# Routed experts of a gated two-layer block: expert blocks loaded transposed as fp16 halves, three sets of PSUM banks, spacing steps left out between scatters, and a new written order

## The reference

```
x = x + tanh(gx0) * decayed_scan(ln(x) * ctx * ctx)              # "A", by one matmul with a decay matrix
x = x + tanh(gf0) * (ln(x) @ W.T + top-1 of 4 low-rank adapters)  # "B"
x = x + tanh(gx1) * sigmoid_attention(ln(x), ctx) @ Wo            # "C", 16 heads of 16 features
x = x + tanh(gf1) * moe(ln(x))                                    # "E"
# moe: logits = x2 @ router_w (8 experts); each token goes to its best 2 experts;
#      h = gelu(row @ w_in[e] + b_in[e]);  y = h @ w_out[e] + b_out[e];  y is weighted and added
```

## Time and profile before

| | us |
|---|---|
| median of three runs | 473.06 |
| lowest and highest | 472.47, 476.5 |
| the profiled execution, device time | 474.49 |
| its span, first to last instruction | 472.6 |
| busy in the span: PE, DVE, ACT, POOL | 394.9, 368.8, 331.4, 268.7 |

### The profile page before, as it was taken

One profiled execution on the slowest core, in us unless ns is written; L12 is line 12 of the kernel. 1 busy time (PEld: TensorE's weight loads), 2 busy tenths in 40 slices (PEclk: granted clock), 3 DMA queues, 4 the chain that ended last, 5 costly groups with the idle time before them and its releaser, 6 DMA issues.

```text
span 472.6 us, 13099 instructions
## 1 busy us (share of the span) xinstructions
PE 394.9 (84%) x4092; PEld 308.3 (65%) x4092; DVE 368.8 (78%) x1416; ACT 331.4 (70%) x671; POOL 268.7 (57%) x313
## 2 busy tenths in 40 slices
PE   2758899998999989999899987789559999979850
PEld 1536667776776777677686765568438897967740
DVE  2888888998988889899789786367655667779994
ACT  2855788898889889898879877566706666646640
POOL 2522112545454364626545565769988888888870
PEclk9998999999999999999999999899959999999996
DMA  7245576664565555875553774624335569396985
GB/s 242 83 139 163 180 214 179 196 181 141 177 213 170 166 171 167 221 204 184 180 174 111 223 220 121 198 68 130 101 126 143 170 175 332 116 341 251 323 275 204
DMA packets 69500, 87.10 MB, mean 184 GB/s; under 512 B 9485, under 2 KB 55290, under 8 KB 69306
## 3 DMA queue, kind: packets, MB, share of 16 engines
q1 hardware_dynamic: 60074, 65.81, 46.7%
q0 software_dynamic: 6816, 18.65, 10.8%
q10 hardware_dynamic: 2544, 1.81, 1.2%
HBM read 51.07 MB, written 35.18 MB: 182 GB/s over the span
## 4 chain that ended last, share of the span: by engine, by line
PE 42%; POOL 17%; issue 14%; DVE 10%; DMA 8%; ACT 6%; ACTq 0%; POOLq 0%; DVEq 0%; SPq 0%
PE ps_J L1650 12%; PE ps_F L1650 6%; POOL store_y L771 6%; DMA store_y<-y_out,y_row 6%; PE ps_O L1764 5%; PE ps_T L1659 5%; POOL store_x L765 5%; PE ps_S L1751 5%; POOL pause_t L778 5%; PE ps_R L1689 2%; PE ps_O L1775 2%; PE ps_G L1650 2%; DMA temp_t<-in_temp 1%; DVE y_out L2934 1%; DVE xb_lo L2903 1%
## 5 line engine op out<-in xcount | busy, mean ns | idle before, releaser
L771 POOL DMA_INDIRECT store_y<-y_out,y_row x78 | 81.4, 1044 | 21.8 <-issue 16.5
L765 POOL DMA_INDIRECT store_x<-xn_E,slot_u x64 | 68.0, 1063 | 26.5 <-DVE slot_u L2633 13.6
L1089 ACT ACTIVATE prob<-ps_S 128x512 f32<-128x512 f32 x128 | 72.4, 594 | 12.7 <-PE ps_S L1751 10.0
L778 POOL TENSOR_TENSOR pause_t<-half_ones,minus_half 128x2 f32<-128x2 f32 x71 | 54.7, 770 | 1.9
L1751 PE MATMUL ps_S<-q_stack,k_stack 128*128 128x256 f16 x256 | 44.5, 276 | 5.9 <-issue 3.8
L2922 DVE TENSOR_TENSOR h_lo<-h_f,h_hi 128x512 f16<-128x512 f32 x39 | 26.9, 689 | 21.0 <-ACT h_hi L1173 9.4
L1650 PE MATMUL ps_J<-wout_hi,h_hi 128*128 x112 | 31.2, 278 | 14.3 <-DVE y_out L2934 10.9
L1764 PE MATMUL ps_O<-prob,v_wide 128*32 128x128 f32 x1024 | 41.0, 279 | 1.1 <-ACT prob L1089 0.5
L1165 ACT ACTIVATE h_f<-ps_F,bin_t 128x256 f32<-128x256 f32 x56 | 23.4, 470 | 24.5 <-PE ps_F L1650 18.9
L751 POOL TENSOR_TENSOR rstd_C<-var_C,minus_half 128x2 f32<-128x2 f32 x16 | 12.1, 759 | 40.4 <-DVE var_C L2412 40.4
L1650 PE MATMUL ps_F<-xb_hi,win_hi 128*128 128x256 f16 x112 | 31.7, 283 | 3.9 <-DVE xb_lo L2903 3.3
(11 more groups left out here) (301 smaller groups left out, 1399.5 us busy)
## 6 DMA issues: line engine op xcount, KB each, us to landing
parts_scratch<-parts SPq DMA_DIRECT2D x32, 256.0 KB
k_stack<-parts_scratch SPq DMA_DIRECT2D x64, 128.0 KB
q_stack<-parts_scratch SPq DMA_DIRECT2D x128, 64.0 KB
xb<-store_x SPq DMA_DIRECT2D x30, 257.0 KB
y_got<-store_y SPq DMA_DIRECT2D x14, 512.0 KB
c_in<-in_ctx SPq DMA_DIRECT2D x16, 256.0 KB
x_in<-in_x SPq DMA_DIRECT2D x16, 256.0 KB
store_x<-zeros SPq DMA_DIRECT2D x15, 257.0 KB, 4.6
```

The lines of the kernel that those rows point to most:

```text
L765: pool.indirect_dma_start(store_x, bass.IndirectOffsetOnAxis(slot_u[q][:, at:at + 1], 0), xn_e[q][:, at, :], None).then_inc(s_scat[q], 16)
L771: pool.indirect_dma_start(store_y, bass.IndirectOffsetOnAxis(y_row[n][:, b:b + 1], 0), y_out[n][:, b, :], None).then_inc(s_y_kept[n], 16)
L778: pool.tensor_tensor(pause_t[:, :], half_ones[:, :], minus_half[:, 0:2], ALU.pow).then_inc(s_set_p, 1)
L1089: act.activation(prob[m % PROBS][:, 2 * n:2 * n + 2, :, :], bank_s[n], ACT.Sigmoid, scale=float(HD) ** -0.5).then_inc(s_prob[n], 1)
```

## The change

**Rows as fp16 parts.** xn_E keeps its 1028-byte rows, but now 512 fp16 values (256 hi, 256 lo) stand in them in place of 256 fp32 values, and the row number stays in the last column. ScalarE's `rows_hi(p)` takes the place of its `normed_e(p)` (same elements, fp16 out). VectorE gets a new `normed_e(p)`, the fp32 rows once per token, into a single buffer xn_f that `transpose_e` reads. GpSimd gets `rows_lo(p)`, 1024 elements per partition, and every scatter waits for it:

```diff
+            def rows_lo(p):
+                pool.wait_ge(s_rows_hi, 2 * p + 2)
+                pool.wait_ge(s_xn["E"], 2 * p + 2)
+                pool.tensor_tensor(e_lo[p % 2], xn_f[:, :, :].unsqueeze(2).broadcast_to([128, 2, TOP, D]), e_hi[p % 2],
+                                   ALU.subtract).then_inc(s_rows_lo, 1)
...
+            def normed_e(p):
+                q = p % 2
...
+                dve.wait_ge(s_rstd["E"], p + 1)
+                need(dve, s_t["E"], p)
+                need(dve, s_rows_lo, p)
+                for b in range(2):
+                    dve.tensor_scalar(xn_f[:, b, :], xs[:, 2 * p + b, :], mv["E"][q][:, b, 0:1], rstd["E"][q][:, b:b + 1],
+                                      ALU.subtract, ALU.mult).then_inc(s_xn["E"], 1)
```

**Transposing block loads.** `load_block` issues two transfers; `transpose_block`, `copy_hi` and `copy_lo` are gone, and `layer1` reads the loaded tile:

```diff
-                sp.dma_start(xb[n][:, :, :], store_x[bass.ds(row_at(i, 0), BLK), :]
-                             .rearrange("(p b) c -> p b c", b=SUB))\
-                    .then_inc(s_xb[n] if n < XB else s_late[(n - XB) // GROUP], 16)
+                at, done = row_at(i, 0), s_xb[n] if n < XB else s_late[(n - XB) // GROUP]
+                sp.dma_start(xb[n][:, :, :], store_x16[bass.ds(at, BLK), 0:2 * D], transpose=True).then_inc(done, 16)
+                sp.dma_start(row_no[n][:, :, :], store_x[bass.ds(at, BLK), D - 1:WIDE].rearrange("(b p) c -> p b c", b=SUB))\
+                    .then_inc(done, 16)
```

**Spacing steps.** From the first `keep_block` on, 6 of 43 are left. The new order on GpSimd there:

```diff
+            keep_block(1, 0)
+            keep_block(1, 1)
+            rows_lo(15)
+            keep_block(2, 0)
+            keep_block(2, 1)
+            keep_block(3, 0)
+            scatter(15, 3)
+            scatter(15, 0)
+            long_pause()
+            scatter(15, 1)
+            keep_block(3, 1)
+            keep_block(4, 0)
+            long_pause()
+            long_pause()
+            keep_block(4, 1)
...
+            keep_block(7, 0)
+            scatter(15, 2)
+            long_pause()
+            keep_block(7, 1)
```

More of the change, by code:

```diff
@@ L413, in build, with last_at @@
         block = st.enter_context(nc.Block())
+        store_x16 = store_x.bitcast(F16)
         def side(i):
-            return 0 if i <= EARLY else (i - EARLY) % 2
+            return i % HB
+        def last_at(k):
+            return max(i for i in range(TILES) if side(i) == k)
         def home(i):
@@ L718, in _ @@
             stack_keys(15)
+            keep_parts("q", 15)
             load_block(0)
+            stack_queries(15)
             load_block(1)
[L721 to L732, removed]
+            load_block(2)
@@ L1637, in _ @@
-            for b in range(2):
-                keep_batch(NP - 1, b)
+            gelu(8)
+            hidden_hi(8)
+            gelu(9)
+            hidden_hi(9)
+            gelu(10)
+            hidden_hi(10)
+            gelu(11)
+            hidden_hi(11)
+            gelu(12)
+            hidden_hi(12)
+            gelu(13)
+            hidden_hi(13)
+            gelu(14)
+            hidden_hi(14)
+            gelu(15)
+            hidden_hi(15)
+            gelu(16)
+            hidden_hi(16)
@@ new lines, in _ @@
+            gelu(17)
+            hidden_hi(17)
+            gelu(18)
+            hidden_hi(18)
+            gelu(19)
+            hidden_hi(19)
+            gelu(20)
+            hidden_hi(20)
+            gelu(21)
+            hidden_hi(21)
+            gelu(22)
+            hidden_hi(22)
+            gelu(23)
+            hidden_hi(23)
+            gelu(24)
+            hidden_hi(24)
+            gelu(25)
+            hidden_hi(25)
+            gelu(26)
+            hidden_hi(26)
+            gelu(27)
@@ L1854, in layer1 @@
                                  first_lo[:, bass.ds(at + (D * k + 128 * m), 128)]) for k in range(KT)],
[L1855 removed]
+                               [(tile[:, k, :], tile[:, KT + k, :]) for k in range(KT)])
                 if m == KT - 1:
@@ L3953, in _ @@
             take_rows(9)
+            take_rows(10)
+            add_bias(8)
+            take_rows(11)
+            next(final)
+            hidden_lo(11)
             next(final)
@@ L3981, in _ @@
-            for n in range(TILES + 1 - ADD_AT, NP):
-                add_pair(n)
+            next(final)
+            next(final)
+            add_bias(9)
+            add_bias(10)
+            hidden_lo(12)
+            next(final)
+            next(final)
+            take_rows(12)
+            take_rows(13)
+            hidden_lo(13)
+            add_bias(11)
+            hidden_lo(14)
+            add_bias(12)
+            take_rows(14)
+            take_rows(15)
+            add_bias(13)
@@ new lines, in _ @@
+            next(gates)
+            take_rows(21)
+            take_rows(22)
+            hidden_lo(22)
+            hidden_lo(23)
+            add_bias(21)
+            add_bias(22)
+            next(gates)
+            take_rows(23)
+            take_rows(24)
+            hidden_lo(24)
+            add_bias(23)
+            next(gates)
+            hidden_lo(25)
+            next(gates)
+            add_bias(24)
+            hidden_lo(26)
+            next(gates)
+            next(gates)
+            take_rows(25)
@@ new lines, in _ @@
+            hidden_lo(27)
+            take_rows(26)
+            take_rows(27)
+            take_rows(28)
+            next(gates)
+            add_bias(25)
+            add_bias(26)
+            hidden_lo(28)
+            hidden_lo(29)
+            next(gates)
+            add_pair(0)
+            add_bias(27)
+            add_pair(1)
+            add_bias(28)
+            take_rows(29)
+            take_rows(30)
+            hidden_lo(30)
+            hidden_lo(31)
+            add_pair(2)
+            add_bias(29)
```

820 lines of the change are left out of this document (562 added, 258 removed).

## The result

The changed kernel takes 488.59 us (487.19 to 491.82, four runs) beside 473.15 us for the kernel before on the same chip: ratio 1.0321, with a 95% interval of 1.025 to 1.0392. It is slower by 3%, where 454 us was forecast.

A forecast was written before the change was run, and what follows sets the result against it. TensorE was taken to bound the pairs, GpSimd the tiles. 472.6 - 24 + 2 + 2 + 5 = 457.6, then -4: span 453.6, device 455.5, about 454 us on the median; range 440 to 472.

The forecast's parts named there:

- the pair part: In the pairs: VectorE's new instructions and GpSimd's `rows_lo` fall mostly in rests; +2 us, bounds 0 and +14.
- Rival (b): In the pairs: 14 `rows_lo` each delay a root by 1 us, giving the gain back, 468 us; chance 0.09.
- The step of GpSimd's pace: In the tiles: without spacing steps GpSimd needs 2.6 us a tile, stores 1.27 to 1.3 us apart.
- The transposing load: Block loads on the transfer engines: 1.5 us in place of 0.7, +0.8 a block; bounds of one load 0.7 and 4.8.
- the last 15 tiles: Tiles that carry the outputs: 3.0 us each against GpSimd's 2.6, 12 x 0.4 = +5 us, bounds 0 and +12.
- the -4: In the tiles: most of GpSimd's 5.2 us of waits for y_out given back by lighter TensorE and VectorE tiles.
- The steps themselves: From the first `keep_block` on, 37 of 43 spacing steps go, 0.65 us each: -24 us, all on the path.
- Rival (c): In the tiles: small descriptors need the time anyhow, stores stay 1.6 us apart, only waits go: 470 us; chance 0.06.
- the end behind the last store: Landing, last loads, adds and store after the last output store: nothing changes, 11.5 us.
- pair 15's later scatters: Scatters standing later among the tiles; tile 16 needs them all and could be late: 0, bound +5.
- its +2: The last `rows_lo`, that of pair 15, lies among the output stores: +2 us.
- Rival (a): Transfer engines from tile 0 on: slow transposing loads, losing from 1.9 us each; at 4.8 us about 541 us; chance 0.14.

The follow-up runs named there:

- b_with_fill: Kernel before plus four GpSimd fills of 128x512 fp16, no operand read, at each of the 16 `rows_lo` places: 486.22 us, ratio 1.0164.
- b_with_one: Kernel before plus two one-operand GpSimd multiplications by a constant, 128x512 each, at each of the 16 `rows_lo` places: ratio 1.0389.
- p_with_steps: Changed kernel with plain block loads, one spacing step put back between the two stores of each of tiles 7 to 35: 493.75 us, ratio 1.0421.

## Why the prediction was wrong

**The step that failed is the pair part, +2 us within 0 and +14.** Its instruction was sized right (2.0 us taken, 2.07 measured), and so was `normed_e` (0.3 taken, 0.41 measured, inside its bounds). Its effect was priced as GpSimd's time in GpSimd's rests. The first store came 23.0 us late, beyond the bound. Rival (b) named the place (a root delayed by half of each `rows_lo`) but not the size. Two things were missed. GpSimd's time in the pairs isn't free at 49% busy, since its roots stand in the loop: 0.32 us are lost for each us in b_with_fill and in b_with_one, which is 8 us for the 24.8 that twelve `rows_lo` take ahead of the `rstd_C` of pair 15 (the other four come behind it). And VectorE, at 86% busy, is held while GpSimd reads two operands: 7 to 10 us are left for that of the 14.9 and 17.9 that the two comparisons of the cut subtract on one chip gave. The clocks at pair 15 say 18.7 us: the subtract, and 3.7 to 6.4 for `normed_e` and the new waits. The 4 more at the first store lie behind pair 15 and are less certain: from `rstd_C` of pair 15 to the first store is 42.3 us in the changed kernel and 38.9 to 43.2 in the eight with plain loads and the subtract, 34.9 to 38.3 in the three with the cut one and 38.0 in the kernel before.

The Trainium skill (GPSIMD Engine Reference, Specifications) says that GpSimd shares its SBUF interfaces with VectorE, with contention where VectorE's instruction is in a 2-port mode or has two SBUF inputs. The trace agrees that there is contention, with 187 ns become 594 for the picks, which have two inputs. Here one small instruction with a single input was held for all of GpSimd's 2.07 us too (whether it was in a 2-port mode the trace doesn't say), and GpSimd's own operands count: with one operand the picks stayed at 207 ns. The page's rule speaks against the change, and the prediction didn't weigh it.

**The tiles: 142.5 - 24 + 2 + 5 - 4 = 121.5 us forecast, 133.8 measured, 122.9 with plain loads on one chip.** The step of GpSimd's pace was right in its mechanism: stores 1.26 us apart, tiles every 2.63 us between stalls (394.01 to 418.97, 19 steps from store to store). What failed is SyncE. The transposing load was priced on the transfer engines alone (+0.8 us a block; their share became 0.81 and 1.01, forecast 0.85 to 0.9), and its issue at nothing, 2.1 to 2.4 us a block with the row numbers. The outputs' loads stand behind block 37's (in the kernel before behind the last block's, so not later in the order), thus came at 431.67, and VectorE stood 10.04 us. The prediction listed the last 15 tiles with +5, bounds 0 and +12, and took no wait for the outputs. Nor did the -4 come: GpSimd's waits for y_out, 5.2 us before, are 21.3 us, and 9.4 of them without this stall. That the issue time and the order together make this stall is read from the trace; with transposing loads it wasn't tried with another order, and the plain ones show only that without them it is gone.

**The steps themselves** cost 0.46 to 0.62 us each on the path in p_with_steps, where 0.65 was taken, and in the kernel before 43 of them gave back 12.5 of 28 us, because TensorE's 3.05 us a tile came next. Rival (c) had 470 us for steps that don't cost what they seem; they do cost, until the next engine.

**Right**: the end behind the last store stayed (11.9 for 11.5), and behind pair 15's later scatters TensorE waits 0.45 us for block 16. The last `rows_lo` takes 2.08 us between two stores, at 348.26, as its +2 had it. Rival (a), slow transposing loads, would have needed 1.9 us a block on the transfer engines. From 402 to 421 us they spend 80.2% of 16 x 19 us on nine blocks with their row numbers, 1.7 us a block (1.5 forecast), and their busy time from 300 to 461 is 128 us (125 forecast). So that price was nearly right, though not far from the rival's.

**Open**: why TensorE is fed in bursts in the tiles on some chips, with plain loads, and whether the changed kernel itself would show it there; it was timed on one chip.

## What to carry to other kernels

Price an instruction that is added to a half idle engine by what stands behind it and by what it takes from its neighbour, not by its length in rests: on GpSimd 0.32 us per us here with little contention, 0.51 with a two-operand instruction beside a busy VectorE (14.7 for 29.1), and 0.6 to 0.7 for the changed kernel's subtract (14.9 and 17.9 for 24.8). Price a transfer three times: on the transfer engines, on the queue that issues it, and for what is queued behind it there. And before a change that rearranges much, try its simplest part alone: taking the spacing steps out of the old kernel gave 3.6%, most of the 4% that was forecast for the whole change.

## What was not expected of the hardware

A two-operand subtract on GpSimd held VectorE's 128x2 step to 2.54 us, and a one-operand multiplication of the same shape was slower by itself (1549 ns for 128x512, the subtract 1208) but held VectorE for only 2.9 us in all, the subtract 14.0. A transposing load of 256 rows takes SyncE 1242 ns to issue, a plain one of the same size 550. After a rest of 4 us TensorE's matmuls came 0.21 us apart for 5.7 us. And one kernel with the same pairs took 483.36, 500.14 and 502.63 us on three chips, while the kernel before stayed between 472.56 and 476.97 on them; why is open.
